# A 64-expert layer's slot table, built by one-hot products on TensorE in place of 64 indirect scatters through memory

## What is computed

```python
logits = flat @ router_w.T
_, topk_idx = top_k(logits + router_bias, 4)
topk_w = softmax(logits) at topk_idx, divided by its sum
pos = place of the choice among the choices of its expert, in order of rows
slot = where(pos < 64, pos, dropped)
tok_table[e, slot] = row         # 64 x 64
w_table[e, slot] = share         # 64 x 64
xg = flat[tok_table]
y = (silu(xg @ gate_w.T) * (xg @ up_w.T)) @ down_w.T
out = zeros.at[tok_table].add(y * w_table)
out = out + a shared expert of 2 x 512 hidden numbers over all rows
```

## Time and profile before

| | |
|---|---|
| median of three runs | 2397.96 us (2395.09 to 2401.51) |
| profiled execution, its time | 2416.67 us |
| profiled execution, its span from first to last instruction | 2414.9 us |
| busy in the span: PE, weight loads, VectorE, ScalarE, POOL | 89%, 47%, 56%, 33%, 28% |
| TensorE's granted clock, mean over the span | 0.953 of 2.4 GHz |
| third layer in the span | about 482 to 990 us |

### The profile page before, as it was taken

How to read it: one execution, slowest core, us unless ns; L and a number is a source line. 1 busy time by engine, 2 the same in 40 slices (tenths; PEclk the granted TensorE clock), 3 DMA queues, 4 the chain that set the end, 5 groups by cost and what they waited for, 6 DMA issues and landing times. The chain is left out here.

```text
span 2414.9 us, 30993 instructions
## 1 busy us (share of the span) xinstructions
PE 2156.5 (89%) x10710; PEld 1145.0 (47%) x10711; DVE 1359.7 (56%) x3183; ACT 799.4 (33%) x1325; POOL 679.1 (28%) x944
## 2 busy tenths in 40 slices
PE   9999979879999999889999987478888888879994
PEld 5777748644444444444444443233333333336762
DVE  5867768755121226366676674945656565455443
ACT  5554624420022211234434333423322232023333
POOL 1200015534322321323343433011113121223553
PEclk9999989988999999999999998689999999999997
DMA  7211232270077764353343330300000000065555
GB/s 265 72 36 53 88 126 83 84 286 1 28 229 249 244 206 150 106 125 87 73 93 75 86 67 1 112 3 1 2 18 2 19 28 19 18 197 135 102 96 167
DMA packets 101672, 231.31 MB, mean 96 GB/s; under 512 B 18886, under 2 KB 42614, under 8 KB 94366
## 3 DMA queue, kind: packets, MB, share of 16 engines
q1 hardware_dynamic: 78974, 187.64, 24.9%
q0 software_dynamic: 22560, 41.87, 7.8%
HBM read 170.49 MB, written 63.53 MB: 97 GB/s over the span
## 5 line engine op out<-in xcount | busy, mean ns | idle before, releaser
L2081 DVE CUSTOM_DVE_ANT_0 D_ps<-D_ps,D_mask 128x256 f32<-128x256 f32 (+1 forms) x512 | 186.7, 419 | 68.3 <-PE D_ps L1978 67.1
L1830 POOL TENSOR_SCALAR_AFFINE_SELECT D_probs<-D_probs 128x256 f32<-128x256 f32 x256 | 106.7, 423 | 284.4 <-ACT D_probs L1888 284.2
L1888 ACT ACTIVATE D_probs<-D_ps 128x512 f32<-128x512 f32 (+1 forms) x256 | 125.4, 542 | 163.9 <-PE D_ps L2000 163.8
L3080 DVE TENSOR_REDUCE F_neg_max<-F_ps 128x4 f32<-128x2048 f32 (+1 forms) x64 | 93.9, 1488 | 107.7 <-PE F_ps L2978 101.6
L2830 ACT ACTIVATE F_probs<-F_ps 128x1536 f32<-128x1536 f32 (+1 forms) x48 | 76.4, 1591 | 187.5 <-PE F_ps L2994 187.5
L1379 PE MATMUL C_ps<-C_xT,C_gate_shared 128*128 128x512 f32 x256 | 119.9, 606 | 6.6 <-issue 6.0
L1379 PE MATMUL C_ps<-C_xT,C_up_shared 128*128 128x512 f32 x256 | 118.5, 604 | 3.7 <-issue 3.7
L1391 PE MATMUL C_ps<-C_down_shared,C_hs 128*128 128x512 f32 x256 | 115.5, 601 | 2.3 <-DVE C_hs L1558 2.1
L1978 PE MATMUL D_ps<-D_k_stack,D_q_stack 96*128 96x256 bf16 (+1 forms) x512 | 92.6, 266 | 8.6 <-DVE D_maxima L2081 7.3
L1228 POOL DMA_INDIRECT expert_sums<-C_y,C_of_slot x32 | 50.3, 1571 | 173.5 <-ACT C_y L1295 103.1
L2711 POOL TENSOR_SCALAR_AFFINE_SELECT F_probs<-F_probs 128x512 f32<-128x512 f32 x64 | 41.1, 654 | 179.9 <-ACT F_probs L2830 179.9
(11 more groups left out here) (549 smaller groups left out, 4861.6 us busy)
## 6 DMA issues: line engine op xcount, KB each, us to landing
C_ring<-moe_experts_dram SPq DMA_DIRECT2D x32, 1536.0 KB
qk_parts<-D_parts SPq DMA_DIRECT2D x32, 384.0 KB, 2.5
expert_sums<-A_zeros SPq DMA_DIRECT2D x1, 8192.0 KB
C_ring<-expert_sums SPq DMA_DIRECT2D x5, 1536.0 KB, 9.9
D_q_stack<-qk_parts SPq DMA_DIRECT2D x16, 384.0 KB, 4.9
D_k_stack<-qk_parts SPq DMA_DIRECT2D x16, 384.0 KB, 7.7
B_w<-ctxT_dram SPq DMA_DIRECT2D x1, 4096.0 KB, 15.9
B_c<-ctx_dram SPq DMA_DIRECT2D x4, 1024.0 KB, 7.5
```

Of the source, the lines that this page charges most:

```text
L1830: last = nc.gpsimd.affine_select(now[:, :, 0:P], now[:, :, 0:P], [[0, 2], [1, P]], ALU.is_ge, 0.0, base=0, channel_multiplier=-1)
L1888: nc.scalar.activation(probs[at % 2][:, 2 * pair:2 * pair + 2, 0:w], ps[:, 4 + unit % 3, :].rearrange("p (h q) -> p h q", h=2)[:, :, 0:w], ...
L2081: last = nc.vector.tensor_tensor_reduce(now, now, mask[:, first:256], 1.0, -3e38, ALU.add, ALU.max, maxima[n % 2][:, head, t:t + 1])
L3080: last = nc.vector.tensor_reduce(neg_max[n % 2][:, :, t], ps[:, 0:GROUP, at:at + w], AX_X, ALU.max, negate=True)
```

## The change

The tensor `slots`, its clearing, the 64 scatters, the wait for them and the load of `of_slot` go. In their place, per group of four tiles, VectorE forms for each of the 16 choices of a row two one-hot patterns: which of 128 slots of a pair (`slot_hot`, 128 columns), and which of 32 pairs, multiplied by three values (row of the sums plus 1, and the share's high and low part; `pair_vals`, 3 x 32 columns). TensorE adds up 16 products of 128 columns of weights by 96 moving columns in one bank of PSUM (`slots_of(b)`), VectorE adds the result to `table` (`keep_slots(b)`), and after the last group three vector instructions and one more make `of_slot` (`finish_slots`). The bank is that of the odd down products, hence two waits on `slots_kept` in `shared_step`. `slot_hot` and `pair_vals` lie in the room of the gathered rows. `count_up` grows from 64 to 128 columns.

```diff
@@ TensorE @@
+            def slots_of(b):
+                pe.wait_ge(hot_ready, b + 1)
+                if b >= 1:
+                    pe.wait_ge(slots_kept, b)
+                if b >= 2:
+                    pe.wait_ge(added, KF)
+                for j in range(CHOICES):
+                    last = nc.tensor.matmul(ps[:, 3, 0:3 * PAIRS], slot_hot[:, j, :],
+                                            pair_vals[:, j].rearrange("p v n -> p (v n)"), start=(j == 0), stop=(j == CHOICES - 1))
+                last.then_inc(slots_filled, 1)
...
+                    if c in (1, KF + 1):
+                        pe.wait_ge(slots_kept, c // KF * 2 + 2)
...
                 if n == 1:
                     places(1)
+                    slots_of(0)
                 if n == 2:
                     logits(2)
+                if n == 3:
+                    slots_of(1)
...
+                if n == 8:
+                    slots_of(2)
                 if n == 9:
                     places(3)
+                if n == 11:
+                    slots_of(3)
@@ VectorE, end of share_out @@
-                nc.vector.tensor_tensor(entry[:, tiles, :, 1].rearrange("p t k -> p k t"), half[:],
-                                        twice[:, tiles].unsqueeze(1).to_broadcast([P, K_C, GROUP]), ALU.bitwise_or)
-                nc.vector.scalar_tensor_tensor(out=entry[:, tiles, :, 2].bitcast(F32).rearrange("p t k -> p k t"), in0=share[:],
-                                               scalar=0.5, in1=total[:].unsqueeze(1).to_broadcast([P, K_C, GROUP]),
-                                               op0=ALU.mult, op1=ALU.mult)
-                steps.after(nc.vector.tensor_scalar(sloti[:], sloti[:], P - 1, None, ALU.bitwise_and))
-                steps.after(nc.vector.scalar_tensor_tensor(out=sloti[:], in0=sloti[:], scalar=float(PAIRS),
-                                                           in1=pairi[:], op0=ALU.mult, op1=ALU.add))
-                nc.vector.tensor_tensor(address[:, b], sloti[:], drop[:], ALU.add).then_inc(address_ready, 1)
+                nc.vector.tensor_copy(lowf[:], lowi[:])
+                nc.vector.tensor_tensor(rowi[:], half[:], twice[:, tiles].unsqueeze(1).to_broadcast([P, K_C, GROUP]), ALU.bitwise_or)
+                nc.vector.tensor_tensor(pairf[:], pairi[:], drop[:], ALU.add)
+                steps.after(nc.vector.scalar_tensor_tensor(out=share[:], in0=share[:], scalar=0.5,
+                                                           in1=total[:].unsqueeze(1).to_broadcast([P, K_C, GROUP]),
+                                                           op0=ALU.mult, op1=ALU.mult))
+                nc.vector.tensor_scalar(rowf[:], rowi[:], 1.0, None, ALU.add)
+                steps.after(nc.vector.tensor_copy(share_hi[:], share[:]))
+                if b >= 1:
+                    dve.wait_ge(slots_filled, b)
+                steps.after(nc.vector.tensor_tensor(share_lo[:], share[:], share_hi[:].bitcast(F32), ALU.subtract))
+                nc.vector.tensor_tensor(slot_hot, count_up[:].unsqueeze(1).to_broadcast([P, CHOICES, P]),
+                                        per_slot(lowf).to_broadcast([P, CHOICES, P]), ALU.is_equal)
+                steps.after(nc.vector.tensor_tensor(pair_hot, count_up[:, 0:PAIRS].unsqueeze(1).to_broadcast([P, CHOICES, PAIRS]),
+                                                    per_slot(pairf).to_broadcast([P, CHOICES, PAIRS]), ALU.is_equal))
+                for v, value in enumerate((per_slot(rowf), per_slot(share_hi).bitcast(F32), per_slot(share_lo).bitcast(F32))):
+                    last = nc.vector.tensor_tensor(pair_vals[:, :, v, :], pair_hot, value.to_broadcast([P, CHOICES, PAIRS]), ALU.mult)
+                last.then_inc(hot_ready, 1)
+            def keep_slots(b):
+                dve.wait_ge(slots_filled, b + 1)
+                filled = ps[:, 3, 0:3 * PAIRS].rearrange("p (v n) -> p v n", n=PAIRS)
...
+                    nc.vector.tensor_tensor(table[:], table[:], filled, ALU.add).then_inc(slots_kept, 1)
...
@@ VectorE, order: keep_slots(0) after step 2, (1) after step 3, (2) after step 9, (3) and finish_slots after step 11 @@
...
@@ SP and POOL @@
-            sp.wait_ge(scattered, 16 * K_C * TILES)
-            sp.dma_start(of_slot[:].rearrange("p n o -> p (n o)"), slots.rearrange("(p n) o -> p (n o)", p=P)).then_inc(slots_in, 16)
...
-            for b in range(B):
-                pool.wait_ge(address_ready, b + 1)
-                for t in range(GROUP):
-                    for k in range(K_C):
-                        pool.indirect_dma_start(slots, bass.IndirectOffsetOnAxis(ap=address[:, b, k, t:t + 1], axis=0),
...
-            pool.wait_ge(slots_in, 16)
+            pool.wait_ge(slots_ready, 1)
```

More of the change, by code:

```diff
@@ L1109, in sems @@
             return [sem(f"{name}{j}") for j in range(n)]
-        slots = nc.dram_tensor("slots", (E_C * CAP, 3), I32).ap()
         ps = ctx.enter_context(nc.psum_tensor("C_ps", [P, 8, 512], F32))
@@ L1121, in moe_layer @@
         before, ones = sb("before", [P, P], BF16), sb("ones", [P, P], BF16)
-        router, count_up, bias = sb("router", [P, KD, E_C]), sb("count_up", [P, E_C]), sb("bias", [P, E_C])
+        CHOICES = K_C * GROUP
+        slot_hot = nc.alloc_sbuf_tensor_at("C_slot_hot", [P, CHOICES, P], F32R, offset=place_xg).ap()
+        pair_vals = nc.alloc_sbuf_tensor_at("C_pair_vals", [P, CHOICES, 3, PAIRS], F32R, offset=place_xg + 4 * CHOICES * P).ap()
+        router, count_up, bias = sb("router", [P, KD, E_C]), sb("count_up", [P, P]), sb("bias", [P, E_C])
         myself, of_slot = sb("myself", [P, TILES], I32), sb("of_slot", [P, PAIRS, 3], I32)
-        empty = y[1][:, 0:PAIRS * 3].bitcast(I32).rearrange("p (n o) -> p n o", o=3)
-        entry = sb("entry", [P, TILES, K_C, 3], I32)
         biased, expd = sb("biased", [P, GROUP, E_C]), [sb(f"expd{j}", [P, GROUP, E_C]) for j in (0, 1)]
         chosen, picked = (sb(n, [P, K_C, GROUP, E_C]) for n in ("chosen", "picked"))
+        pair_hot = picked[:, 2:4].rearrange("p k t e -> p (k t e)").rearrange("p (c n) -> p c n", n=PAIRS)
         mask, so_far = sb("mask", [P, GROUP, E_C]), sb("so_far", [P, E_C])
@@ L1132, in moe_layer @@
         share, place, kept, slotf, drop = (sb(n, [P, K_C, GROUP]) for n in ("share", "place", "kept", "slotf", "drop"))
-        sloti, pairi, half = (sb(n, [P, K_C, GROUP], I32) for n in ("sloti", "pairi", "half"))
+        sloti, lowi, pairi, half, rowi = (sb(n, [P, K_C, GROUP], I32) for n in ("sloti", "lowi", "pairi", "half", "rowi"))
+        lowf, pairf, rowf = (sb(n, [P, K_C, GROUP]) for n in ("lowf", "pairf", "rowf"))
+        share_hi, share_lo = (sb(n, [P, K_C, GROUP], F32R) for n in ("share_hi", "share_lo"))
         twice = sb("twice", [P, TILES], I32)
-        address = sb("address", [P, B, K_C, GROUP], I32)
+        table, vacant = sb("table", [P, 3, PAIRS]), sb("vacant", [P, PAIRS])
         power, stats, mv, rstd, shift = sb("power", [P, GROUP]), sb("stats", [P, 6]), sb("mv", [P, TILES, 2]), sb("rstd", [P, TILES]), sb("shift", [P, TILES])
@@ L1167, in _ @@
             sp.dma_start(ones32, d["ones"]).then_inc(consts_in, 16)
-            sp.dma_start(count_up[:], d["count_up"][:, 0:E_C]).then_inc(consts_in, 16)
+            sp.dma_start(count_up[:], d["count_up"]).then_inc(consts_in, 16)
             for b in range(1, B):
@@ L1495, in choose @@
                 steps.after(nc.vector.tensor_copy(at[:], best_at[:, :, 0:K_C].rearrange("p t k -> p k t")))
-                steps.after(nc.vector.tensor_tensor(chosen[:], count_up[:].unsqueeze(1).unsqueeze(1).to_broadcast(per_choice),
+                steps.after(nc.vector.tensor_tensor(chosen[:], count_up[:, 0:E_C].unsqueeze(1).unsqueeze(1).to_broadcast(per_choice),
                                                     at[:].unsqueeze(3).to_broadcast(per_choice), ALU.is_equal))
@@ new lines, in finish_slots @@
+            def finish_slots():
+                nc.vector.tensor_tensor(of_slot[:, :, 2].bitcast(F32), table[:, 1, :], table[:, 2, :], ALU.add)
+                steps.after(nc.vector.tensor_scalar(vacant[:], table[:, 0, :], 0.0, 2.0 * TOKENS + 1.0, ALU.is_equal, ALU.mult))
+                steps.after(nc.vector.scalar_tensor_tensor(out=of_slot[:, :, 1], in0=table[:, 0, :], scalar=-1.0, in1=vacant[:],
+                                                           op0=ALU.add, op1=ALU.add))
+                nc.vector.tensor_scalar(of_slot[:, :, 0], of_slot[:, :, 1], 1, TOKENS - 1, ALU.logical_shift_right, ALU.bitwise_and
+                                        ).then_inc(slots_ready, 1)
@@ L1616, in _ @@
             shared_step(2)
+            keep_slots(0)
             pick(2)
             shared_step(3)
+            keep_slots(1)
             choose(2)
@@ L1628, in _ @@
             shared_step(9)
+            keep_slots(2)
             share_out(3)
@@ L1631, in _ @@
                 shared_step(n)
+                if n == 11:
+                    keep_slots(3)
+                    finish_slots()
```

(2 more changed lines are left out.)

32 lines of the change are left out of this document (16 added, 16 removed).

## The result

| | before | after |
|---|---|---|
| median | 2397.96 us (2393.84 to 2401.59) | 2412.15 us (2401.07 to 2415.46) |
| ratio to before, 95% interval | | 1.0049 (1.0035 to 1.0062) |
| profiled execution, time and span | 2416.67, 2414.9 us | 2412.52, 2410.8 us |

The change makes the kernel slower by half a percent; 2408.2 us was forecast. The measured 2412.15 lies inside the stated range (2400.5 to 2417) and just above the narrower one that the forecast gave itself (up to 2412). The times of after lie in two groups, about 2401 to 2405 and 2411 to 2415.5 us.

The account below looks back on a forecast made before the run. TensorE's stream was taken to bound the layer: products 8.2, wait at `places(1)` 1.6 and at `slots_of(3)` 0.4 add 10.2 us to 2397.96, giving 2408.2 us. Range 2400.5 to 2417, its own narrower one 2405.2 to 2412.

Parts of the forecast that it names:

- What bounds the layer: From 509 to 905 us TensorE's own work sets the layer's time; the table was ready more than 15 us too early.
- The slow stretch as an event of one execution: TensorE's slow 534 to 559 us in before's profile, a 19.4 us loss, belongs to that execution and isn't in the median.
- Rival 1: Faster: the scatters cause the slow stretch of 534 to 559 us in every execution; 2388.8 us, chance 0.11.
- What goes costs nothing: Removing 64 scatters, 81 us of POOL on no path, gains nothing; their slack was some 15 us.
- The products, forecast at 8.2 us: 64 added F32R products on TensorE's path, 0.115 us each plus about 0.2 us a group: 8.2 us more.
- The 0.2 us a group for the first load: On TensorE, each group's new products pay about 0.2 us for first load and change of bank, hidden in a running stream.
- Rival 2: No change that can be told: new products cost 0.06 us each, TensorE's waits 2.0; 6.7 us more, 2404.7 us, chance 0.22.
- The estimate of 6.0 us: Alternative price of TensorE's new products from the skill page's 81 ns: 5.2 + 0.8 = 6.0 us instead of 8.2.
- VectorE's tail, forecast at 5.5 us a group: VectorE's new tail in `share_out` ends 5.5 us later each group, so TensorE loses 1.6 us at `places(1)`.
- The 0.4 us for `slots_of(3)`: After step 11, TensorE's last group of table products waits some 0.4 us for VectorE's `share_out(3)`.
- The sum, forecast at 10.2 us: In the 20 early steps, 8.2 + 1.6 + 0.4 = 10.2 us more; 2408.2 us, 0.43% slower.
- Rival 3: Slower: VectorE's tail 2 us a group dearer, clock falls after pauses, 2414.1 us; or 0.23 a product, 2415.5; chance of either 0.15.

Follow-up runs that it names:

- the one with scatters beside: 64 indirect DMAs of 128 x 12 bytes put back on POOL, into unread memory, in the changed kernel with five dense products; 2403.16 us, ratio 1.0025.
- doubled: Each group's 16 table products issued twice, on the changed kernel with five dense products ahead of the layer's first transposes; 2413.63 us, ratio 1.0062.

## Why the prediction was right, point by point

**What bounds the layer.** Right. TensorE's stream sets the time, and the table was ready too early: the gathers left 39.4 us ahead of the turn, and the turn moved by what TensorE's stream gained in work.

**The slow stretch as an event of one execution.** Right as to its being no part of the comparison: it is in none of the other profiles, neither in the five of kernels that form the table by scatters (step 0 to first turn 118.85 to 118.89 us in each), nor in the one with scatters beside, nor in those without scatters. The times agree: of the hundred times of before in four series the highest is 2405.04 us. The clock is not what began it. Two stretches of before, and the record behind the pause:

```profile
532.00:534.00 2.00, 1.49 (x14) 1.54 (x14) 0.33 (x2) 0.00 (x0) 1.39 (x3) 1.00 0.01 1
534.00:536.00 2.00, 0.22 (x1) 0.27 (x1) 0.40 (x1) 0.00 (x0) 1.70 (x2) 0.88 0.03 1
```

```profile
535.03 0.22 PE L1351 MATMUL C_ps<-C_router,C_xT 128*128 128x64 f32 x1 [1.53 <-issue]
```

TensorE stopped at 533.5 us with the clock still at 1.00, and from then on its records came 1.4 to 2.1 us apart, with idle time between that waits for nothing in the trace; the lower clock followed. Why they came so late stays open, and that the second group's scatters, which ran at the same time, had a part in this one execution isn't excluded: six other profiles with 64 scatters don't have it. Rival 1, which needs it in every execution, would have given 2388.8 us and is out. The loss was 20.0 us (138.83 - 118.85), not 19.4.

**What goes costs nothing.** Right within 0.5 us for the scatters. The table's clearing and its load weren't tested by themselves.

**The products, forecast at 8.2 us.** 7.2 to 7.4 us. The 0.115 us from the logits' row was right, 0.113 in the kernel after and 0.112 doubled. The 0.2 us a group for the first load was wrong: 16 products take 1.81 us from the first's start to the start of the next step's first record, so the first load is hidden as in a stream. Rival 2's price of 0.06 belongs to bfloat16, where it is 0.043. The Trainium skill, TensorE: Matmul & The Clock Gate, section Weight-path perf modes, has fast loads for 128 weights of every type but FP32; in this program F32R weights load in 186 to 192 ns, as F32 does, and bf16 in 98. As far as the loads' durations tell, the trace disagrees with that rule for F32R. The estimate of 6.0 us, which took the 81 ns of section Back-to-back issue gap, was too low by 1.2.

**VectorE's tail, forecast at 5.5 us a group.** In the kernel after it runs, as I count it, from 519.83 to 525.63 us (timeline of VectorE):

```profile
519.83 0.17 DVE L1547 CAST C_lowf<-C_lowi 128x16 f32<-128x16 int32 x1
...
520.78 2.29 DVE L1559 TENSOR_TENSOR C_slot_hot<-C_count_up,C_lowf 128x2048 fp32r<-128x2048 f32 x1
522.99 0.68 DVE L1561 TENSOR_TENSOR C_picked<-C_count_up,C_pairf 128x512 f32<-128x512 f32 x1
...
525.63 0.69 DVE L1595 SCALAR_TENSOR_TENSOR C_gu_s<-C_th_s,C_ps 128x512 f32<-128x512 f32 x1
```

That is 5.8 us, of which 0.95 for the short operations (the eighth of them stands ahead of it, 0.1 us more) and 4.85 for the five long ones (5.1 forecast), where the old tail took 0.76 from the same point: 5.0 to 5.1 more instead of 5.5, so the waits came out smaller: 1.03 us at `places(1)` instead of 1.6, under 0.1 at `slots_of(3)` instead of 0.4. The step that failed slightly is the distance of the unordered long operations: the last three follow each other at 0.61 us, not 0.71, and the short ones in front take 1.0, not 1.2. The 0.4 us for `slots_of(3)` was also a slip: the forecast's own terms, 1.1 + 12.9 against 13.9, leave 0.1.

**The sum, forecast at 10.2 us.** The mechanism gives less: 127.40 - 118.85 = 8.55 us between the untouched kernels' traces, 7.4 to 7.8 where the clock was held up, 7.6 us in the medians with five dense products and 8.35 with four. (The lengths forecast for this stretch, 118.5 and about 128.5 us, rest on a slip: 138.8 - 19.4 is 119.4. Measured are 118.85 and 127.40.) The means of the untouched kernels differ by 10.2. That the forecast of 2408.2 meets the mean of 2408.5 is thus partly luck: 1.7 us too much in the terms, and about as much missing for what the untouched kernels differ by beyond them. The clock could fill the gap, in part by falls, which the forecast gave only to pauses of over 2 us (1.7 us in one of the two profiles of after), in part by a longer stretch at the lower level before step 0. That it does isn't shown.

**Rival 3.** Its mechanism is real, its condition wasn't met here: the tail wasn't dearer than thought, and the waits stayed at 1 us. When VectorE's tail was made 2.3 us longer a group, it did what the rival said, twice the delay and the clock on top: 8.35 us. The length of the pause alone doesn't decide: behind a pause of 1.02 us the clock fell once for 1.6 us, while behind 1.03, 1.04, 1.12 and 1.26 at the same place it didn't, nor behind 2.02 us before step 0 in after with four dense products (1.00 from 509.6 to 516 us). What does decide I can't say from the runs.

**What I hadn't seen.** But for the slow stretch, the largest difference between two profiles of the same kernel lies before step 0, and the profile of before had the short case: 21.0 us from the first transposes to step 0. In the second profile of the same kernel it is 27.9. I read the stretches only from 509 us on.

## What to carry to other kernels

Before moving work from one engine to a busier one, look for who waits for it: 81 us of POOL's time were free, and 7.3 us of TensorE's were not. Price a short product on TensorE by a row of products as short and of the same type (0.115 and 0.113 us here for 64 and for 96 columns), not by its columns, and choose the type accordingly: one-hots are exact in bfloat16, and the products then took 0.043. And where a layer starts behind a pause of TensorE with small transposes, try a few dense products in the pause: five, 7 us of work in a pause of 12.9, made the kernel before 4 to 5 us faster by the two ratios (2394.25 and 2394.84 us), the only version here that is faster than both kernels clear of noise.

## What the runs showed of the hardware that I had not expected

The granted clock can stay at 1.2 GHz for 25 us though TensorE is at work all the time: 25.40 of 27 us busy at 0.51, with transposes and router products of 64 columns, in the kernel after. With four dense products ahead it rose as the last of them ran. Stretches of before with those four, which run from 482.34 to 488.7 us; TensorE's busy time first:

```profile
480.00:484.00 4.00, 1.66 (x2) 0.83 (x3) 0.00 (x0) 0.00 (x0) 0.54 (x4) 0.50 0.09 17
484.00:487.00 3.00, 3.00 (x5) 1.25 (x4) 0.00 (x0) 0.00 (x0) 0.00 (x0) 0.50 0.98 356
487.00:490.00 3.00, 2.76 (x12) 1.47 (x12) 0.37 (x5) 0.80 (x2) 0.00 (x0) 0.86 0.98 296
490.00:500.00 10.00, 8.32 (x70) 7.50 (x69) 4.33 (x18) 4.34 (x11) 0.00 (x0) 1.00 1.01 379
```

The same transposes and router products then ran at 1.00 to the end. So what the engine did before such a stretch can set the clock of the whole stretch. It isn't needed for a high one: the first profile of before had 1.00 from 492 to 534 us without them. The Trainium skill, TensorE: Matmul & The Clock Gate, section The HAM clock gate, has the lower clock as the resting state that activity releases; the rows agree in that the pause of 12.8 us leaves the lower clock, and show that work by itself doesn't always release it: 25 us of transposes and router products behind the pause ran at 0.51, behind four dense products at 1.00.

A product of 128x128 F32R weights by 96 columns is one record and costs 0.113 us in a stream; in bfloat16 0.043. A VectorE operation with a broadcast operand takes the same with an F32R as with a bfloat16 output, 2.29 us for 2048 elements; for 512 elements it is 0.68 to 0.69 with either of them and with an F32 output.
